# A graph network's prologue re-ordered: edge ends read as contiguous runs, layer norm on ScalarE, another way to the block table

## What is computed

```python
h = maximum(layernorm(x), 0)
# layer 0: attention over the edges in both directions (400000 ends)
ngl, ngr = h @ Wl.T, h @ Wr.T                   # 4 heads of 16
score = (att * leaky_relu(ngl[src] + ngr[dst])).sum(-1)
alpha = softmax of score over the edges with one src
out = segment_sum(ngr[dst] * alpha, src)
x = x + (gelu([out, h] @ W1.T + b1) @ W2.T + b2)
h = maximum(layernorm(x), 0)
# layer 1: sum of messages, a small network, a batch norm
agg = segment_sum(h[src] + edge_attr, dst)
x = x + batchnorm(relu(agg @ W1 + b1) @ W2 + b2)
```

## Time and profile before

| | |
|---|---|
| time, median of 3 runs | 7274.71 us (7274.49 to 7275.52) |
| the profiled execution: its time | 7273.11 us |
| its span, first to last instruction | 7271.3 us |
| PE, PEld busy | 4213.4, 4021.1 us (58%, 55%) |
| DVE busy | 4450.5 us (61%) |
| ACT busy | 713.7 us (10%) |
| POOL busy | 4588.8 us (63%) |
| `prepare` | 0 to about 988 us |
| `decode` | about 988 to 1063 us |
| `attention` with its nodes | about 1064 to 5239 us |
| `messages` with its nodes | about 5239 to 7271 us |

### The profile page before, as it was taken

How to read it: one execution, slowest core, us unless ns; L and a number is a source line. 1 busy time by engine, 2 the same in 40 slices (tenths; PEclk the granted TensorE clock), 3 DMA queues, 4 the chain that set the end, 5 groups by cost and what they waited for, 6 DMA issues and landing times. The chain is left out here.

```text
span 7271.3 us, 76898 instructions
## 1 busy us (share of the span) xinstructions
PE 4213.4 (58%) x19023; PEld 4021.1 (55%) x19023; DVE 4450.5 (61%) x7849; ACT 713.7 (10%) x1072; POOL 4588.8 (63%) x4809
## 2 busy tenths in 40 slices
PE   2011115777767777777677777777534444566666
PEld 1011115776766776677677766667433444555665
DVE  9999975666767776776777776768512222222232
ACT  6201100000000000000000000000100000000001
POOL 0000037777777777777777777776177777777774
PEclk9975555555555555555555555555655555555555
DMA  2000014444434444444344444443111111111111
GB/s 37 0 0 0 0 46 125 119 119 116 120 109 125 125 122 119 118 116 117 110 127 124 120 120 118 117 114 113 46 53 53 53 53 53 53 54 54 53 53 30
DMA packets 634439, 600.62 MB, mean 83 GB/s; under 512 B 383267, under 2 KB 389795, under 8 KB 633719
## 3 DMA queue, kind: packets, MB, share of 16 engines
q10 hardware_dynamic: 180384, 320.64, 13.5%
q0 software_dynamic: 153344, 157.33, 10.1%
q1 hardware_dynamic: 300246, 117.47, 6.4%
HBM read 480.76 MB, written 114.19 MB: 82 GB/s over the span
## 5 line engine op out<-in xcount | busy, mean ns | idle before, releaser
L857 POOL DMA_INDIRECT rows<-gr_table,row_of x3192 | 3038.0, 952 | 976.1 <-issue 970.3
L1373 POOL DMA_INDIRECT edge_rows<-h_table,src_sb x1568 | 1481.7, 945 | 531.9 <-issue 474.3
L888 PE MATMUL bank<-terms,hot_sum 128*128 128x68 f32 x6448 | 1466.3, 422 | 586.8 <-DVE acc L1023 583.8
L888 PEld LDWEIGHTS bank<-terms,hot_sum 128*128 128x128 f32 x6448 | 1412.2, 331 | 624.3 <-DVE hot_sum L1044 622.3
L878 PE MATMUL bank<-gl_step,hot_t 128*128 128x64 f32 x6448 | 1458.9, 421 | 228.3 <-DVE hot_t L1012 139.3
L878 PEld LDWEIGHTS bank<-gl_step,hot_t 128*128 128x128 f32 x6448 | 1421.8, 333 | 241.7 <-DVE hot_t L1012 228.0
L1394 PE MATMUL bank<-message,edge_hot 128*128 128x64 f32 x3136 | 714.7, 423 | 879.1 <-DVE message L1456 879.1
L1394 PEld LDWEIGHTS bank<-message,edge_hot 128*128 128x128 f32 x3136 | 683.5, 330 | 910.2 <-issue 910.2
L1456 DVE TENSOR_TENSOR message<-bank,edge_rows 128x512 f32<-128x512 f32 x196 | 135.5, 691 | 1071.4 <-DMA edge_rows<-h_table,src_sb 1068.6
L1064 DVE TENSOR_TENSOR z<-bank,rows 128x512 f32<-128x512 f32 x403 | 277.0, 687 | 732.3 <-DMA rows<-gr_table,row_of 729.6
L698 POOL DMA_INDIRECT rows<-gr_table,row_of x32 | 50.1, 1567 | 957.3 <-DVE row_of L729 947.9
(11 more groups left out here) (267 smaller groups left out, 3348.4 us busy)
## 6 DMA issues: line engine op xcount, KB each, us to landing
place_b<-place_rows ACTq DMA_DIRECT2D x403, 256.0 KB
gr_rows<-rows ACTq DMA_DIRECT2D x403, 256.0 KB, 3.5
rows_again<-gr_rows ACTq DMA_DIRECT2D x403, 256.0 KB
rows<-gr_table,row_of POOLq DMA_INDIRECT x3224
gl_step<-gl_table SPq DMA_DIRECT2D x1612, 32.0 KB
edge<-in_edge_attr SPq DMA_DIRECT2D x97, 512.0 KB, 3.4
edge_rows<-h_table,src_sb POOLq DMA_INDIRECT x1568, 2.4
pen_s<-pen_rows ACTq DMA_DIRECT2D x104, 32.0 KB
```

Source lines behind the costliest of these rows:

```text
L857: pool.indirect_dma_start(rows[k][:, g, :], None, m.gr_table[:, :], bass.IndirectOffsetOnAxis(m.row_of[:, tile:tile + 1], 0)).then_inc(s_g ...
L888: last = pe.matmul(sums_of(r % SUM_SLOTS, g // GROUP_TILES), hot2[r % LAG][:, g, :], by_tile[:, g, :], start=g % GROUP_TILES == 0, stop=g ...
L1373: pool.indirect_dma_start(rows[h % U][:, e, :], None, m.h2_table[:, :], bass.IndirectOffsetOnAxis(m.src[:, tile:tile + 1], 0)).then_inc(s_ ...
```

## The change

- SP first issues four DMAs that read `src` and `dst` as 128 contiguous runs (127 of 1563 ends, 6252 bytes, and one of 1499) into the free buffer `keys[1]`. The loads into `m.src` and `m.dst` stay, behind those of `x`.
- The memsets of `src_f` and `keys[0]` cover only what isn't written later. `bias` is made ahead of the ends.
- Keys are made from the runs on DVE; the casts to `src_f` move to ACT, and the 49 `Sign` passes follow at once there.
- The first layer norm moves to ACT: 49 `Identity` with accumulation, 49 `Identity` with bias, 49 `Square` with accumulation, `Sqrt`, 49 `Relu` with scale; DVE keeps six small operations of it. ACT then does the 13 rounds for `gl` and `gr`. PE waits for the last of them ahead of the sort's turns.
- `span` and the copies of transposed weights move behind `vector_front`. Since the tail columns are kept out, the minimum is one reduction over 97 groups and a small one.
- `blk_i`: each partition compares its 13 groups with all 49 ends, sums up, and a DMA lays the 128 x 13 results in one row. The PE transpose, the four matmuls and the copies of up to 1612 elements on one partition go.
- The stages of the pad columns (`vector_pads`) come behind the block table; the 14 small operations on `spans` and the small rest of the layer norm behind these; then `vector_rest` from stage 10 on.
- In `decode` three of the eight bank copies move from ACT to DVE, `row_of` is made for the first 32 tiles and then for the others, and `pad_f` and the second `seg_i` come after `row_of` instead of before it.

```diff
@@ prepare, SP
+            for dram, run in ((t["src"], runs[0]), (t["dst"], runs[1])):
+                sp.dma_start(run[0:P - 1, :], dram[0:(P - 1) * RUN].rearrange("(p c) -> p c", c=RUN)).then_inc(s_runs, 16)
+                sp.dma_start(run[P - 1:P, 0:LAST_RUN], dram[(P - 1) * RUN:E].rearrange("(o c) -> o c", o=1)
+                             ).then_inc(s_runs, 16)
             sp.wait_ge(s_init, 1)
             load_blocks(sp, m.x, t["x"], s_x)
...
             sp.wait_ge(s_grt, 32)
+            sp.wait_ge(s_block, 1)
+            sp.dma_start(m.blk_i[0:1, :].rearrange("o (p g) -> o p g", p=P), block_of[:, :]).then_inc(s_block_row, 16)
+            sp.wait_ge(s_block_row, 16)
@@ prepare, ACT
+            act.wait_ge(s_runs, 64)
+            act.wait_ge(s_init, 3)
+            for way in range(2):
+                for parts, lo, hi in pieces:
+                    nc.scalar.copy(src_f[0:parts, way * EDGE_COLS + lo:way * EDGE_COLS + hi], runs[way][0:parts, lo:hi]
+                                   ).then_inc(s_cast, 1)
+            act.wait_ge(s_cast, 4)
+            act.wait_ge(s_src_f, 1)
...
+            act.wait_ge(s_x, 32)
+            for b in range(BLOCKS):
+                nc.scalar.activation(gl[:, b, :], m.x[:, b, :], ACT.Identity, accum_out=m.mean[:, b:b + 1]).then_inc(s_ln_sum, 1)
+            act.wait_ge(s_ln_sum, BLOCKS)
+            nc.scalar.mul(m.mean[:, :], m.mean[:, :], -1.0 / D).then_inc(s_ln_mean, 1)
+            act.wait_ge(s_ln_mean, 1)
+            for b in range(BLOCKS):
+                nc.scalar.activation(m.h[:, b, :], m.x[:, b, :], ACT.Identity, bias=m.mean[:, b:b + 1]).then_inc(s_ln_h, 1)
+            for b in range(BLOCKS):
+                act.wait_ge(s_ln_h, b + 1)
+                nc.scalar.activation(gl[:, b, :], m.h[:, b, :], ACT.Square, accum_out=m.var[:, b:b + 1]).then_inc(s_ln_square, 1)
             act.wait_ge(s_var0, 1)
             nc.scalar.activation(m.rstd[:, :], m.var[:, :], ACT.Sqrt).then_inc(s_std0, 1)
+            act.wait_ge(s_ln_rstd, 1)
+            for b in range(BLOCKS):
+                last = nc.scalar.activation(m.h[:, b, :], m.h[:, b, :], ACT.Relu, scale=m.rstd[:, b:b + 1])
+            last.then_inc(s_h, 1)
@@ prepare, PE
-            pe.wait_ge(s_end, 1)
-            pe.transpose(bank[6][0:BLOCKS, 0:P], ends[:, :], m.ident[:, :]).then_inc(s_end_ps, 1)
-            pe.wait_ge(s_past, 1)
-            part = GROUPS // 4
-            for i in range(4):
-                last = pe.matmul(bank[4 + i][:, 0:part], m.ones[0:BLOCKS, :], past[:, i * part:(i + 1) * part],
-                                 start=True, stop=True)
-            last.then_inc(s_past_ps, 1)
+            pe.wait_ge(s_lr, len(rounds))
             sort.tensor(pe)
@@ prepare, DVE
-            dve.memset(src_f[:, :], FAR)
-            dve.memset(m.keys[0][:, :], NO_KEY)
+            dve.memset(m.keys[0][:, 2 * EDGE_COLS:ROW], NO_KEY)
             c.link(dve.memset(m.ones[:, :], 1.0))
-            dve.wait_ge(s_x, 32)
-            layernorm_steps(m, c, dve, m.x, m.h, gl, s_var0, s_std0, 1).then_inc(s_h, 1)
...
+            dve.wait_ge(s_runs, 64)
+            for way in range(2):
+                a, b = runs[way], runs[1 - way]
...
+            dve.wait_ge(s_cast, 4)
+
+            sort.vector_front(dve)
+
+            dve.wait_ge(s_edges, 64)
...
-            dve.wait_ge(s_end_ps, 1)
-            c.link(dve.tensor_copy(end_col[:, :], bank[6][0:BLOCKS, 0:1]))
-            dve.tensor_scalar(past[:, :], iota_group[:, :], end_col[:, 0:1], None, ALU.is_ge).then_inc(s_past, 1)
-            dve.wait_ge(s_past_ps, 1)
-            part = GROUPS // 4
-            for i in range(4):
-                c.link(dve.tensor_scalar(m.blk_f[:, i * part:(i + 1) * part], bank[4 + i][0:1, 0:part],
-                                         float(BLOCKS - 1), None, ALU.min))
-            c.link(dve.tensor_copy(m.blk_i[:, :], m.blk_f[:, :]))
+            c.link(dve.tensor_tensor(past[:, :, :], iota_group[:, :].unsqueeze(2).to_broadcast([P, PART_GROUPS, BLOCKS]),
+                                     ends[:, :].unsqueeze(1).to_broadcast([P, PART_GROUPS, BLOCKS]), ALU.is_ge))
+            c.link(nc_reduce(dve, block_f[:, :], past[:, :, :]))
+            dve.tensor_scalar(block_of[:, :], block_f[:, :], float(BLOCKS - 1), None, ALU.min).then_inc(s_block, 1)
+            sort.vector_pads(dve)
...
+            dve.wait_ge(s_ln_square, BLOCKS)
+            dve.tensor_scalar(m.var[:, :], m.var[:, :], 1.0 / D, LN_EPS, ALU.mult, ALU.add).then_inc(s_var0, 1)
+            dve.wait_ge(s_std0, 1)
...
+            dve.tensor_tensor(m.rstd[:, :], m.rstd[:, :], bias[:, :], ALU.mult).then_inc(s_ln_rstd, 1)
             sort.vector_rest(dve)
@@ Sort
+    def vector_pads(self, dve):
+        self.stages(dve, 1, 7, self.FRONT, self.PADS)
+        self.stages(dve, 8, self.FRONT_STAGES - 1, self.FRONT, ROW - self.FRONT)
@@ decode, ACT
-            for k in range(8):
+            for k in range(BY_ACT):
@@ decode, DVE
+            c.link(dve.tensor_scalar(pad_row[:, :], m.iota_node[:, 0:1], float(BLOCKS * P), None, ALU.add))
+            for k in range(BY_ACT, 8):
+                dve.wait_ge(s_tr, k + 1)
+                squares4 = bank[k][:, :].rearrange("p (j r) -> p j r", j=4)[:, :, 0:rows]
+                dve.tensor_copy(tile_view(key_t, k), squares4).then_inc(s_moved, 1)
+            dve.wait_ge(s_moved, 8)
+            for lo, hi in ((0, FIRST), (FIRST, TILES_UP)):
+                c.link(dve.tensor_single_scalar(pad_t[:, lo:hi], key_t[:, lo:hi].bitcast(I32), NODE_MASK, ALU.bitwise_and))
+                dve.tensor_scalar(m.row_of[:, lo:hi], pad_t[:, lo:hi], pad_row[:, :], None, ALU.min).then_inc(s_row, 1)
             c.link(dve.tensor_scalar(pad_f[:, :], seg_i[:, :], float(NODE_MASK), None, ALU.is_equal))
             c.link(dve.tensor_scalar(seg_i[:, :], key, NODE_BITS, NODE_MASK, ALU.logical_shift_right, ALU.bitwise_and))
-            dve.wait_ge(s_moved, 8)
-            c.link(dve.tensor_scalar(pad_row[:, :], m.iota_node[:, 0:1], float(BLOCKS * P), None, ALU.add))
-            c.link(dve.tensor_single_scalar(pad_t[:, :], key_t[:, :].bitcast(I32), NODE_MASK, ALU.bitwise_and))
-            dve.tensor_scalar(m.row_of[:, :], pad_t[:, :], pad_row[:, :], None, ALU.min).then_inc(s_row, 1)
```

More of the change, by code:

```diff
@@ L117 @@
     pass
[L120 to L137, removed]
 def nc_reduce(dve, out, in_, op=ALU.add):
@@ L263, in prepare @@
     s_init = sem("s_init")
-    s_edges = sem("s_edges")
+    s_runs, s_edges = sem("s_runs"), sem("s_edges")
+    s_cast = sem("s_cast")
+    s_ln_sum, s_ln_mean, s_ln_h, s_ln_square = sem("s_ln_sum"), sem("s_ln_mean"), sem("s_ln_h"), sem("s_ln_square")
+    s_ln_rstd = sem("s_ln_rstd")
+    runs = [m.keys[1][:, way * EDGE_COLS:way * EDGE_COLS + RUN].bitcast(I32) for way in range(2)]
     s_x = sem("s_x")
@@ L327, in _ @@
                 nc.scalar.copy(gr[:, b:b + n, :], terms[:, :, 1, :]).then_inc(s_lr, 1)
[L328 to L333, removed]
             sort.scalar(act)
@@ L362, in _ @@
             pe.wait_ge(s_ident, 2)
-            pieces = (w_l0[:, 0, :], w_l0[:, 1, :], w1_l0[:, 0:D], w1_l0[:, D:2 * D], w2_l0[:, :])
-            for i, w in enumerate(pieces):
+            weights = (w_l0[:, 0, :], w_l0[:, 1, :], w1_l0[:, 0:D], w1_l0[:, D:2 * D], w2_l0[:, :])
+            for i, w in enumerate(weights):
                 last = pe.transpose(bank[4][0:D, i * D:(i + 1) * D], w, m.ident[0:D, 0:D])
             last.then_inc(s_wt_ps, 1)
+            pe.wait_ge(s_cnt, 1)
+            pe.matmul(bank[5][:, 0:BLOCKS], m.ones[:, :], below[:, :], start=True, stop=True).then_inc(s_cnt_ps, 1)
             pe.wait_ge(s_h, 1)
@@ L399, in _ @@
             dve.memset(m.dst[:, FULL_COLS:EDGE_COLS], -1).then_inc(s_init, 1)
+            for way in range(2):
+                dve.memset(src_f[96:P, way * EDGE_COLS + LAST_RUN:(way + 1) * EDGE_COLS], FAR)
+                dve.memset(src_f[0:96, way * EDGE_COLS + RUN:(way + 1) * EDGE_COLS], FAR)
+                dve.memset(m.keys[0][96:P, way * EDGE_COLS + LAST_RUN:(way + 1) * EDGE_COLS], NO_KEY)
+                dve.memset(m.keys[0][0:96, way * EDGE_COLS + RUN:(way + 1) * EDGE_COLS], NO_KEY)
@@ new lines, in _ @@
+            c.link(dve.tensor_scalar(bias[:, :], bias[:, :], 0.5 - P, None, ALU.add))
+            dve.engine_nop().then_inc(s_src_f, 1)
+            dve.wait_ge(s_runs, 64)
+            for way in range(2):
+                a, b = runs[way], runs[1 - way]
+                base = way * EDGE_COLS
+                for parts, lo, hi in pieces:
+                    key = m.keys[0][0:parts, base + lo:base + hi].bitcast(I32)
+                    c.link(dve.scalar_tensor_tensor(key, a[0:parts, lo:hi], NODE_BITS, b[0:parts, lo:hi],
+                                                    ALU.logical_shift_left, ALU.bitwise_or))
+                    c.link(dve.tensor_single_scalar(key, key, KEY_BIT, ALU.bitwise_or))
@@ L406, in _ @@
```

(16 more changed lines are left out.)

95 lines of the change are left out of this document (42 added, 53 removed).

## The result

The changed kernel is slower: 7302.44 us median (7296.31 to 7339.92) against 7274.49 (7272.24 to 7316.13) for the kernel before on the same chip, a ratio of 1.0039 with a 95% interval of 1.002 to 1.0058. The forecast was 7242, 60 us less. The profiled execution has a span of 7299.9 us and a time of 7301.72, against 7271.3 and 7273.11: 28.6 us more in both.

A forecast was written before the change was run, and what follows sets the result against it. It took DVE in `prepare`, a DVE/POOL stretch in `decode`, then POOL's gathers as the bound. The terms -32.1 - 2.1 + 1.3 = -32.9 us took 7274.7 to 7242, range 7234 to 7250.

The forecast's parts named there:

- What bounds the kernel: DVE in `prepare`, a DVE/POOL stretch in `decode`, then POOL, whose gathers in both layers keep about 1.25 us pitch.
- The start of the sort: In `prepare`, DVE begins the sort at about 14.0 instead of 46.10, 32.1 us earlier; bounds 13.6 and 19.3.
- the runs' landing: In `prepare`, the contiguous loads of `src` and `dst` are in at 7.5 us, ahead of DVE's key work.
- Between the front and the pads, and the layer norm's rest: In `prepare`, DVE from `vector_front` to the pads' stages: moved, cheaper and added work sums to -2.1 us.
- Does ACT keep up?: In `prepare`, ACT is ready for counts, layer norm and sort turns, with 46 us of cover at the tightest place.
- rival 3: ACT becomes the bound of `prepare` through 245 small layer norm records; 7293 at 0.6 us each; chance 0.07.
- `decode`: In `decode`, POOL starts 4.8 us earlier, but seven early gathers are slow; this part loses 1.3 us.
- the reading: In `decode`, gathers started within a DVE operation on SBUF tiles get on only at its end, 0.12 or 0.82 behind.
- the head start: In `decode`, POOL's first early gather starts 4.8 us earlier because the first part of `row_of` is ready sooner.
- Rival 1: In `prepare`, the runs land late because ACT's weights and `x` share DMA engines; sort at 19.3, 7247; chance 0.12.
- Rival 2: In `decode`, the early gathers run free of DVE's operations; 1.3 + 4.8 us better, 7236; chance 0.12.
- Rival 4: Behind the barrier after `decode`, the head start is given back; excluded by POOL's fixed pitch, no chance given.

The follow-up runs named there:

- the first experiment: Changed kernel with each 127-row load of `src` and `dst` cut into 112 and 15 rows; 7242.58 us median, ratio 0.9954.
- the last experiment: Kernel with 112 and 15 rows and the earlier `decode`, plus 98 repeated pairs of `Square` with accumulation on ACT; 7238.73 us, single execution.
- old order: Changed kernel with 112 and 15 rows, `decode` as before the change, DVE's operations behind `row_of` in 512-column pieces; 7223.94 us median, ratio 0.993.
- new order: Changed kernel with 112 and 15 rows, its own `decode`, DVE's operations behind first `row_of` part in 512-column pieces; 7256.56 us median, ratio 0.9948.

## Why the prediction was wrong, point by point

**What bounds the kernel**: right. The pitch of the gathers is unchanged, and the four parts of the table add up to 28.67 us, where the span grew by 28.6.

**The start of the sort**: this step failed, in its first term. I put the runs' landing at 7.5 us, between 6 from `place_rows` and 12.9 from `x`. It was 68.05. Both rows are of transfers over 128 partitions, and the new one has 127; I compared bytes and sizes of pieces, and not the shape. So the 12.9 us from `x` were no upper bound for it. No row of before shows a transfer over one engine at a large size, and there the bound should have come from below: what a single engine moves. With 16 engines the transfer measured 10.9 and with 14 engines 9.99, inside the bounds, and later than my value by 3.4 and 2.5 us: this smaller error of the same term stands beside the large one.

The keys were 3.2 us a way (68.05 to 74.49 are 6.44). ACT's casts were not late in any kernel.

**Between the front and the pads, and the layer norm's rest**: -2.40 against -2.1, so the prices from shapes not in the trace (the comparison and the reduction of 637 elements, 0.82 us each against 0.8) held:

```profile
273.01 0.82 DVE L476 TENSOR_TENSOR past<-iota_group,ends 128x637 bf16<-128x637 f32 x1
273.87 0.82 DVE L124 TENSOR_REDUCE block_f<-past 128x13 f32<-128x637 bf16 x1
```

**Does ACT keep up?** Yes. In the changed kernel the late start moved each appointment, but the kernels without it show the same: ACT waits 63.1 us (126 and 1 partitions) and 64.0 us (112 and 15, old `decode`) for DVE ahead of the root, and PE's first turn of the sort is at 397.15 in the first experiment, the forecast's 394 plus the 3.4 us of the later start. The activations with accumulation, the unknown of rival 3, are these:

```profile
L327 ACT ACTIVATE gl<-x_in 128x64 f32<-128x64 f32 x49 | 11.7, 248 | 0.0
L327 ACT ACTIVATION_READ_ACCUMULATOR gl<-x_in 128x1 f32 x49 | 9.6, 195 | 0.0
L332 ACT ACTIVATE h_sb<-x_in,mean 128x64 f32<-128x64 f32 x49 | 11.8, 332 | 0.0
```

Their means are above my 0.22 and 0.186, but they overlap: one pair starts 0.24 us behind the last. The cover at the root was 65.6 us, and the sum of squares done three times over, in the last experiment, left 41.3. Rival 3 falls.

**`decode`**: right in kind and 1 us short in size. I had foretold seven slow gathers instead of five; the timeline after has seven (first row: DVE's copies of the last banks):

```profile
1020.58 2.20 DVE L751 COPY key_t<-bank 128x404 f32<-128x404 f32 x3 [2.86 <-PE bank L730]
...
1023.59 3.47 POOL L721 DMA_INDIRECT rows<-gr_table,row_of  x1 [754.46 <-DVE row_of L755]
1027.35 4.23 POOL L721 DMA_INDIRECT rows<-gr_table,row_of  x1 [0.30 <-issue]
1031.89 6.36 POOL L721 DMA_INDIRECT rows<-gr_table,row_of  x1 [0.30 <-issue]
1038.55 4.86 POOL L721 DMA_INDIRECT rows<-gr_table,row_of  x1 [0.30 <-issue]
1043.71 6.05 POOL L721 DMA_INDIRECT rows<-gr_table,row_of  x1 [0.30 <-issue]
1050.06 3.45 POOL L721 DMA_INDIRECT rows<-gr_table,row_of  x1 [0.30 <-issue]
1053.82 3.96 POOL L721 DMA_INDIRECT rows<-gr_table,row_of  x1 [0.30 <-issue]
1058.08 0.94 POOL L721 DMA_INDIRECT rows<-gr_table,row_of  x1 [0.30 <-issue]
```

The third ends at 1038.25, the last slow one at 1057.78. DVE's rows beside them:

```profile
1031.50 4.43 DVE L758 SCALAR_TENSOR_TENSOR seg<-seg_i,keys 128x4096 f32<-128x4096 int32 x1
1035.84 2.29 DVE L759 TENSOR_SCALAR seg_i<-seg_i 128x4096 int32<-128x4096 int32 x1
...
1053.43 3.52 DVE L773 TENSOR_TENSOR place<-place,keys 128x3232 f32<-128x3232 f32 x1
```

The third gather ends 0.12 us behind L759 (1038.13) and the last slow one 0.83 behind L773 (1056.95), as the reading says. By the Trainium skill, page "SBUF — State Buffer", section "A bandwidth-pool intuition that's wrong (but worth ruling out)", right below the box that the prediction names ("blocked until DVE-end + ~115 ns"), the trace agrees for the gathers that end 0.12 us behind a `tensor_scalar`; the 0.83 us are not in that figure. What was short is the head start, 3.5 us (8.35 from DVE's first operation in `decode` to the first gather, against 11.86 before) and not 4.8. DVE waited 2.86 us for the transposes, which took 6.28 us instead of 5.80, and its three copies (2.20 us together) end 1.4 us behind the last of them, where I had allowed 0.55.

**The rivals.** Rival 1 named late runs, by shared engines, and its price was 5 us; the kernel without the fault is in between (sort at 17.36, my value 14.0, its bound 19.3). Rival 2, free early gathers, falls in all kernels with whole operations. Rival 4 stays excluded: behind the barrier nothing was given back. What was missing is a rival for a transfer that runs on fewer engines, and my "slower" had only ACT in it. With the sort at 17.36, the forecast's other terms give -29.5 at the first gather of `attention`; measured in the first experiment were -29.3 (1034.68 against 1064.00).

**Luck.** The median of the first experiment, 7242.58, is the forecast's 7242 to within a microsecond, and that is in part luck. At the first gather of `attention` it had 29.3 us of the forecast's 32.9; in the shorter executions it is 32.6 us faster than before (7241.4 against 7274.0). The 3.3 us between the two come from behind that gather, where the forecast had nothing, and are not explained.

## What to carry to other kernels

Ask of every new DMA first how many engines its outermost dimension can use, the largest divisor up to 16: 127 rows take 66 us where 112 and 15 take about 9. A row of another transfer prices it only if that count is the same; bytes and piece sizes don't show it. And where GpSimd's gathers run beside VectorE, the length of VectorE's single operations is what they pay: the same work in pieces of 512 columns brought the first gather of `attention` 16 us (old order) and 21 us (new order) forward.

## What was not expected of the hardware

- **The issue of a small transfer can stand behind a loaded DMA engine.** SP's issue of a single row took 29.89 us, behind 127 rows on the same engine, and the load of `x` stood behind it in the program (timeline of SP, above). That the full queue is the reason is my reading. Loads on many engines hold SP up too: in the first experiment the issue of the second transfer of `x` lasted 10.43 us.
- **One DMA engine** moved 26 to 27 GB/s in pieces of 6 KB and 9 GB/s in pieces of 64 bytes; four moved 99. With 126 rows the window shows 287 GB/s and with 112 and 15 up to 297, both with other loads beside.
- **Two lengths of `attention_nodes`.** The profiles of longer executions (four of the ten) differ from the others in the clock that TensorE was granted in this block. A window of the block in the profiled execution of before, and one of the first experiment:

```profile
5180.00:5200.00 20.00, 20.00 (x107) 11.59 (x107) 15.55 (x31) 9.01 (x16) 5.23 (x3) 1.00 0.00 1
```

```profile
5150.00:5190.00 40.00, 39.49 (x110) 20.10 (x111) 15.80 (x27) 12.03 (x20) 9.46 (x3) 0.50 0.14 40
```

The share 1.00 is the level of 2.4 GHz and 0.50 that of 1.2. In the one PE does 107 multiplications in 20 us, in the other 110 in 40. POOL's wait for the end of the block is 54.5 us in the one and 94.4 in the other. In all kernels PE had worked at 0.50 in `attention`, and in the 40 us ahead of these windows it was busy for 29.30 us (in which the clock rose) and for 29.80 (in which it didn't); what decides it stays open. Of all executions the longer kind came up in 11 of 55 of before (with its loads cut or not) and in 22 of 59 of the kernels with the change in some form, so that a tie to the change can't be excluded, though the experiments here can't show one. One execution of before is 8 us above the shorter ones, and the profiled one of the first experiment is 54 above: it has 40 us more in `attention_nodes` and most of the rest in `attention`.
- **`attention` varies by a few microseconds** from its first gather to `attention_nodes` (4111.8 us before, 4113.2 after, and from 4106.6 to 4120.0 in the other kernels, one profile of each). In the four kernels without the fault that were timed repeatedly, the gain of the shorter executions is 3 to 6 us larger than the shift at the first gather: 32.6 against 29.3, 36.7 against 31.2, 52.3 against 47.1 and 55.9 against 50.2. Why is open.
